# Top-4 routing by top-8 instructions, its marks and ranks moved to GpSimd, the shared expert moved between the first maxima, and the first attention unit's operands loaded early

## The reference, cut to what matters

```python
xn = layernorm(x)
s = attention_block(xn)            # two 8-head attentions of head width 8, then a feed-forward
# gate over 32 experts in 8 groups of 4
scores = softmax(xf @ wg.T)                                # (4096, 32)
keep_g = the 4 groups with the largest group maximum
masked = where(keep_g, scores, -inf)
_, idx = top_k(masked, 4);  w = scores[idx] / (sum + 1e-9)
oh = one_hot(idx.reshape(-1), 32)
pos = (cumsum(oh, axis=0) * oh).sum(-1) - 1                # rank of a token within its expert
keep = pos < cap                                           # cap = 640 rows per expert
y = scatter-add over experts of ((silu(xe@w1) * (xe@w3)) @ w2) * w
z = (silu(xf @ sw1) * (xf @ sw3)) @ sw2                    # the shared expert, all tokens
x = x + s * silu(y + z)
```

## Time and profile before

| what | us |
|---|---|
| median of 3 runs | 1955.45 (1953.72 to 1958.94) |
| the profiled execution, its own time | 1959.3 |
| its span, first to last instruction | 1957.4 |
| first chunk of maxima, PE | 117.6 |
| first score of the attention, PE | 148.65 |
| last exponentials of the attention, about | 1335 |

### The profile page before, as it was taken

The page is one execution under the profiler, slowest core; times in us unless marked ns, Lnnn a source line. Parts: engine busy times, 40 slices in busy tenths (PEclk is TensorE's granted clock), DMA queues, the critical chain, the costliest instruction groups (busy, mean ns, idle before and its releaser), DMA issues.

```text
span 1957.4 us, 41209 instructions
## 1 busy us (share of the span) xinstructions
PE 1756.8 (90%) x15446; PEld 661.8 (34%) x15446; DVE 1684.3 (86%) x2501; ACT 1522.4 (78%) x2880; POOL 422.0 (22%) x676
## 2 busy tenths in 40 slices
...
DMA packets 156349, 146.35 MB, mean 75 GB/s; under 512 B 39882, under 2 KB 135117, under 8 KB 156002
## 3 DMA queue, kind: packets, MB, share of 16 engines
...
## 4 chain that ended last, share of the span: by engine, by line
PE 70%; DVE 10%; ACT 9%; POOL 5%; issue 5%; DMA 1%; SPq 0%; POOLq 0%; DVEq 0%; ACTq 0%
PE PS L1770 28%; PE PS L1796 16%; PE PS L1754 10%; POOL VP L1628 4%; ACT probs L1243 4%; PE PS L1839 4%; ACT SG L1232 2%; PE PS L2034 2%; PE PS L2016 2%; DVE mxp L808 1%; PE PS L1826 1%; DVE YM L892 1%; PE PS L2106 1%; PE PS L2037 1%; PE PS L2019 1%
## 5 line engine op out<-in xcount | busy, mean ns | idle before, releaser
L808 DVE TENSOR_REDUCE mxp<-PS 128x1 f32<-128x1024 f32 x1024 | 1169.1, 1212 | 16.9 <-PE PS L1754 13.4
L1243 ACT ACTIVATE probs<-PS 128x512 f32<-128x512 f32 x2048 | 1095.8, 596 | 86.7 <-PE PS L1796 38.8
L1770 PE MATMUL PS<-probs,VH 128*32 128x256 f32 x8192 | 655.5, 392 | 35.5 <-ACT probs L1243 21.2
L1754 PE MATMUL PS<-stacks 48*128 48x512 bf16 x2048 | 407.2, 384 | 15.9 <-DVE mxp L808 15.9
L1796 PE MATMUL PS<-stacks 51*128 51x512 bf16 x2048 | 414.1, 388 | 0.0
L1770 PEld LDWEIGHTS PS<-probs,VH 128*32 128x32 f32 x8192 | 162.4, 108 | 469.3 <-ACT probs L1243 240.1
L1796 PEld LDWEIGHTS PS<-stacks 51*128 51x128 bf16 x2048 | 110.0, 93 | 424.3 <-ACT probs L1243 391.1
L1628 POOL DMA_INDIRECT VP<-oe_d,ROWI x128 | 132.8, 1037 | 215.6 <-DMA oe_d<-stacks 172.5
L1597 POOL DMA_INDIRECT xe_d<-xn_s,rows_s x128 | 126.5, 988 | 215.1 <-PE PS L1770 180.4
L1575 POOL CAST spl<-nmx 128x8 bf16<-128x8 f32 x64 | 12.0, 188 | 577.7 <-DVE nmx L803 428.2
L820 DVE TENSOR_TENSOR stacks<-stacks,PS 128x640 f32<-128x640 f32 x32 | 26.2, 819 | 112.4 <-ACT stacks L1281 112.4
...
## 6 DMA issues: line engine op xcount, KB each, us to landing
...
o_d<-SG SPq DMA_DIRECT2D x256, 32.0 KB, 1.9
...
```

The costliest lines, as they stand in the source:

```text
L808: v.tensor_reduce(mxp[:, n // 2, n % 2:n % 2 + 1], MXB[n % 2].rearrange("p a c -> p (a c)"), X_AX, ALU.max).then_inc(mx_done, 1)
L1243: act.activation(probs[:, at:at + 512], PS[:, bank_of(u, e), :], ACT.Exp, scale=float(1.0 / np.sqrt(np.float32(DK)))).then_inc(exp_done, 1)
L1754: mm = pe.matmul(MXB[n % 2][:, i, :], QS[w][o:o + MAXROWS, (n // 2) * P:(n // 2 + 1) * P], KS[w][o:o + MAXROWS, key:key + 512], start=True ...
L1770: mm = pe.matmul(OB[32 * jg:32 * jg + 32, c:c + 256], VH[w][:, kt, :], probs[:, at:at + 256], start=(kt < 2 and half == 0), stop=(kt >= TC ...
```

## The change

The four rounds over 128x1024 become one `max` (the 8 largest, in order) and one `max_index` (their places) for each of the 32 tiles. The tiles of these are spread over the eight remainders. The third part of the keys goes from POOL to DVE (`third`), and its wait is the new semaphore `part2k`. Marks, counts and rows go to POOL, in steps between the `largest` calls of units 0 to 8; the prefix counts on PE (`ranks`, four bf16 matmuls) go into unit 5 at step 21, in the place of one chunk, with an ACT copy behind them. One instruction less of the row work stays on DVE in the experts (a reciprocal and a product of the weights). PE's shared expert is cut into 24 steps, each behind one of the first 26 chunks, and its inputs use the PSUM banks 0 and 1. For unit 0, SP loads the queries after the fourth block's stores, and ACT itself issues the key loads between block 6 and block 7; the units 1, 2 and 3 and the late constants are loaded later, at three places of SP's order.

```diff
+    def store_parts(j):
+        hold(part2k, j + 1)
         hold(part2, j + 1)
         for parts, src, stored in ((ql_d, QPARTS, ql_st), (kl_d, KPARTS, kl_st)):
             hold(stored, 48 * j)
             for lv in range(3):
                 sp.dma_start(parts[lv, :, j * 512:(j + 1) * 512], part(src, lv, j % 4)).then_inc(stored, 16)
...
+    def load_first_queries():
+        hold(ql_st, 48 * NB // 2)
+        for o in (0, 64):
+            row = o
+            for r in range(3):
+                n = 3 - r
+                sp.dma_start(QS[0][row:row + n * DK, :], ql_d[r, 0:DK, 0:S].unsqueeze(0).broadcast_to([n, DK, S])).then_inc(qk_ld[0], 16)
+                row += n * DK
+    for j in range(NB // 2):
+        store_parts(j)
...
+    for j in range(NB // 2, NB):
+        store_parts(j)
...
-    for u in range(4):
-        load_unit(u, u // 2, u % 2, u)
+    load_unit(1, 0, 1, 1)
...
     load_max(0, 0, 0, 0)
+    load_unit(2, 1, 0, 2)
...
+            if isinstance(k, int) and u == 0:
+                load_unit(3, 1, 1, 3)
+            if isinstance(k, int) and u == 1:
+                load_late()
...
+        after(v, part2k, j - 1)
...
+    def third(j):
+        v.wait_ge(part1, j + 1)
+        v.tensor_tensor(part(KPARTS, 2, j % 4), KREST[j % 2], part(KPARTS, 1, j % 4), ALU.subtract).then_inc(part2k, 1)
...
+    remainder(0)
     link(v.tensor_tensor(rank, rank, io[:, 0:NG].unsqueeze(1).broadcast_to([P, NT, NG]), ALU.subtract))
...
+    remainder(1)
     link(v.tensor_tensor(g4(M), g4(SC), keep, ALU.min))
...
-    for k in range(KTOP):
-        ek, wk = (t[:, :, k:k + 1].broadcast_to([P, NT, E]) for t in (EK, WK))
-        link(v.tensor_reduce(WK[:, :, k:k + 1], M.unsqueeze(2), X_AX, ALU.max))
-        link(v.tensor_tensor(hots[4], M, wk, ALU.is_equal))
-        link(v.tensor_tensor(hots[4], hots[4], exps, ALU.mult))
-        remainder(2 * k)
-        link(v.tensor_reduce(EK[:, :, k:k + 1], hots[4].unsqueeze(2), X_AX, ALU.min))
-        link(v.tensor_tensor(hots[k], exps, ek, ALU.is_equal))
-        link(v.scalar_tensor_tensor(flat(M), flat(hots[k]), -4.0, flat(M), ALU.mult, ALU.add))
-        if k < KTOP - 1:
-            remainder(2 * k + 1)
-    v.tensor_scalar(SEL, M, -2.5, None, ALU.is_lt).then_inc(sel_done, 1)
-    remainder(NB - 1)
...
-    v.wait_ge(lg_ready, 3)
-    link(v.tensor_copy(T1, bank(2)))
-    v.sem_inc(sums_read, 1)
-    src, dst = T1, SC
-    step = 1
-    while step < NT:
-        link(v.tensor_copy(dst[:, 0:step, :], src[:, 0:step, :]))
-        link(v.tensor_tensor(dst[:, step:NT, :], src[:, step:NT, :], src[:, 0:NT - step, :], ALU.add))
-        src, dst, step = dst, src, 2 * step
...
-    for k in range(KTOP):
-        link(v.tensor_tensor(T1, hots[k], M, ALU.mult))
-        link(v.tensor_reduce(ROW[:, :, k:k + 1], T1.unsqueeze(2), X_AX, ALU.add))
...
+    for j in range(2, NB):
+        third(j - 2)
+        if j < 4:
+            for t in range(NT // 2 * (j - 2), NT // 2 * (j - 1)):
+                ins = v.max(top8[:, t, :], M[:, t, :])
+            link(ins)
+        else:
+            for t in range(NT // 4 * (j - 4), NT // 4 * (j - 3)):
+                v.max_index(place8[:, t, :], top8[:, t, :], M[:, t, :])
+        remainder(j)
+    third(NB - 2)
...
+            if n == 0 and uu == 0:
+                third(NB - 1)
...
+        v.wait_ge(rows_done, 1)
+        link(v.reciprocal(s0, s0))
+        link(v.tensor_tensor(WK[:, :, :], WK[:, :, :], s0.unsqueeze(2).broadcast_to([P, NT, KTOP]), ALU.mult))
...
+    def load_first_keys():
+        act.wait_ge(kl_st, 48 * NB // 2)
+        for o in (0, 64):
+            row = o
+            for r in range(3):
+                n = 3 - r
+                act.dma_start(KS[0][row:row + n * DK, :], kl_d[0:n, 0:DK, 0:S]).then_inc(qk_ld[0], 16)
+                row += n * DK
...
+        if j == NB - 2:
+            load_first_keys()
...
+            if u == RANK_UNIT and e == RANK_EXP:
+                act.wait_ge(lg_ready, 3)
+                act.activation(place.rearrange("p t e -> p (t e)"), MXB[RANK_CHUNK % 2].rearrange("p a c -> p (a c)"), ACT.Copy).then_inc(sums_read, 1)
...
-        for left, parts in ((QREST, QPARTS), (KREST, KPARTS)):
-            ins = pool.tensor_tensor(part(parts, 2, j % 4), left[j % 2], part(parts, 1, j % 4), ALU.subtract)
-        ins.then_inc(part2, 1)
...
+        pool.tensor_tensor(part(QPARTS, 2, j % 4), QREST[j % 2], part(QPARTS, 1, j % 4), ALU.subtract).then_inc(part2, 1)
...
+    def chosen(k):
+        rlink(pool.tensor_tensor(hot_t, numbers, EK[:, :, k:k + 1].broadcast_to([P, NT, E]), ALU.subtract))
+        rlink(pool.tensor_scalar(hots[k], hot_t, 0.0, None, ALU.is_equal))
+    def chosen_any():
+        rlink(pool.tensor_tensor(hot_t, hots[0], hots[1], ALU.add))
+        rlink(pool.tensor_tensor(hot_t, hot_t, hots[2], ALU.add))
+        rlink(pool.tensor_tensor(taken.rearrange("p (t e) -> p t e", e=E), hot_t, hots[3], ALU.add))
+        rlink(pool.memset(before[:, 0:E], 0.0))
+    def counted(half):
+        for t in range(1 + 15 * half, 16 + 16 * half):
+            rlink(pool.tensor_tensor(before[:, t * E:(t + 1) * E], before[:, (t - 1) * E:t * E], taken[:, (t - 1) * E:t * E], ALU.add))
+        if half == 1:
+            pool.sem_inc(cum_done, 1)
+    def fold(src, into):
+        n = E // 2
+        while n > 1:
+            rlink(pool.tensor_tensor(hot_t[:, :, 0:n], src[:, :, 0:n], src[:, :, n:2 * n], ALU.add))
+            src, n = hot_t, n // 2
+        rlink(pool.tensor_tensor(into, hot_t[:, :, 0:1], hot_t[:, :, 1:2], ALU.add))
+    def row_of(k):
+        if k == 0:
+            pool.wait_ge(sums_read, 1)
+        rlink(pool.tensor_tensor(hot_t, hots[k], place, ALU.mult))
+        fold(hot_t, ROW[:, :, k:k + 1])
...
     for u in range(3):
         values(u)
+    for j in range(6):
+        gated_product(j)
     largest(0, 0)
+    for j in range(6, NB):
+        gated_product(j)
+    begin_rows()
...
+    def rows_step(n):
+        if n < KTOP:
+            chosen(n)
+        elif n == KTOP:
+            chosen_any()
+        elif n <= KTOP + 2:
+            counted(n - KTOP - 1)
+        elif 2 * RANK_UNIT + 2 <= n < 2 * RANK_UNIT + 2 + KTOP:
+            row_of(n - 2 * RANK_UNIT - 2)
+        elif n == 2 * RANK_UNIT + 2 + KTOP:
+            end_rows()
     for u in range(3, UNITS // 2):
         values(u)
         largest(u - 3, 1)
+        rows_step(2 * (u - 3))
         largest(u - 2, 0)
+        rows_step(2 * (u - 3) + 1)
...
+    def shared(m):
+        j, step = divmod(m, 3)
+        if step < 2 and j < NB:
+            shared_in(j, step)
+        elif step == 2 and 0 < j < NB:
+            shared_project(j - 1)
+        elif m == CHUNKS + AHEAD - 1:
+            shared_project(NB - 1)
...
+    def ranks():
+        pe.wait_ge(cum_done, 2)
+        pe.wait_ge(mx_done, RANK_CHUNK - 1)
+        for h in range(2):
+            pe.matmul(MXB[RANK_CHUNK % 2][:, h, :], upto16, taken[:, h * 512:(h + 1) * 512], start=True, stop=False)
+            mm = pe.matmul(MXB[RANK_CHUNK % 2][:, h, :], ones16, before[:, h * 512:(h + 1) * 512], start=False, stop=True)
+        mm.then_inc(lg_ready, 1)
...
+    pe.wait_ge(ew_ld[0], 16)
+    pe.wait_ge(v_out, NB)
     for m in range(CHUNKS + AHEAD):
         max_chunk(m)
-        if m == CHUNKS // 2:
-            pe.wait_ge(rows_done, 1)
+        shared(m)
...
+            if u == RANK_UNIT and e == RANK_EXP:
+                ranks()
+            elif u == RANK_UNIT and e == RANK_EXP + 1:
+                pass
+            elif chunk < min(CHUNKS * UNITS, CHUNKS * (u + 1) + AHEAD + CHUNKS * (e + 1) // EXPS):
                 max_chunk(chunk)
```

131 lines of the change are left out of this document (67 added, 64 removed).

## The result

The changed kernel took 1931.56 us (median of 4 executions, 1928.95 to 1936.8), the kernel before 1955.23 us beside it: ratio 0.9874, 95% interval 0.9859 to 0.9889. It is faster by 23.7 us, where 41.8 were forecast, and it lies 1.6 us above the upper end of the range.

The account below looks back on a forecast made before the run. DVE's list and the first maxima were taken to bound the stretch before a full attention. Terms -47.7 + 2.0 + 1.0 + 1.7 + 0.7 - 1.0 + 1.5 = -41.8 us gave a forecast of 1913.5 us, range 1902 to 1930.

Parts of the forecast that it names:

- the landing of the first operands: Before the first chunk: unit 0's key loads land near 70.5, queries near 69, so the first chunk can go at 72.
- Rival (c): Unit 0's loads wait at the end of the stores; the first chunk comes 8 us later, 1921; chance 0.08.
- a cold PE: In the first 26 chunks PE was said to idle no longer, so its clock should be high, over 0.8.
- chunk pitch: In the first 26 chunks, each was taken at 1.20 us against 1.12 before: 25 x 0.08 = +2.0.
- the eighth third: The keys' last subtraction on DVE, between the first two reductions of maxima, was taken to add +1.0 us.
- rival (a): PE paces the first maxima at 1.55 us a chunk, +8.8; with max_index at 0.5 us as well, 1932; chance 0.15.
- The start of the attention: At the first score: ACT's exponential table costs +0.7 us, a warm PE gives -1.0 us.
- DVE's list: From 41.22 to the first reduction: remainders 11.2, thirds 7.0, top-8 instructions 10.2, sum 31.3 us, DVE ready at 72.5.
- Rival (b): Every third finds GpSimd's subtraction just started and waits: +14.6 us, so 1928; chance 0.06.
- the attention's cover: In units 0 to 8, GpSimd's row work of about 67 us, in steps of at most 8, costs nothing.
- (d): GpSimd's 128x1024 instructions cost double and nine steps in units 0 to 8 delay the maxima: +27, 1940; chance 0.06.
- (e): GpSimd's steps stop DVE's reductions in units 0 to 8, up to 67 us, 1980, slower than before; chance 0.03.

Follow-up runs that it names:

- d1: The changed kernel with SP issuing all twelve loads of unit 0 and ACT none: 1931.96 us, ratio 0.9869 to the kernel before.
- k1: The changed kernel with unit 0's loads reading the feature rows outermost and the copies inside: 1929.36 us, ratio 0.9859 to the kernel before.
- w1_warm: The changed kernel with 14 matmuls that nobody reads on PE in front of the first chunk: 1929.73 us, ratio 0.9862 to the kernel before.
- e1_tables: The changed kernel with one-element Silu and Exp instructions so that ACT's tables load ahead: 1929.18 us, ratio 0.9845 to the kernel before.
- p2_best: The changed kernel with rows-outermost loads for unit 0, 10 unread matmuls and both tables ahead: 1920.03 us, ratio 0.9805 to the kernel before.
- a2_again: The changed kernel, unaltered, on another chip: 1933.92 us, ratio 0.9875 to the kernel before.
- p1_best: The changed kernel with rows-outermost loads for unit 0, 14 unread matmuls and both tables ahead: 1994.97 us, ratio 0.986 to the kernel before.
- m1: The changed kernel with rows-outermost unit 0 loads, all from SP, top-8 instructions later, eight shared-expert steps before the first chunk, tables early: 1929.1 us, ratio 0.9856.
- b1: The changed kernel with the early load undone, unit 0 loaded behind all stores, the keys' last third ahead of the first reduction: 1946.39 us, ratio 0.9942.

## Why the prediction was wrong, step by step

**The step that failed: the landing of the first operands.** The prediction had the six key loads land 2 us behind their last issue, at 70.5. The last landed at 76.80, 7.45 us behind the start of the last issue and 7.0 behind its end (69.79). The 2 us are what stores take (2.0 us, the median of the kernel before), which use most of the engines: from 60.00 to 61.70, with stores alone under way, the share is 0.77. These loads use 2 to 3 of 16 (d1), and with the other order of dimensions they land in 4.25 us and the first chunk stands at 72.40 (k1), where the prediction had put it (72). The key stores' landing (65.17, forecast 65) and the end of ACT's issues (4.60 us on its timeline, taken 3.7; ACT is free at 69.9, forecast 68.5) were close. Nothing in the prediction looked at the DMA share of the loads before, though a window of the kernel before shows it, in which nothing but loads of units moved:

```profile
120.00:130.00 10.00, 4.34 (x16) 0.82 (x16) 9.93 (x12) 0.00 (x0) 0.00 (x0) 0.55 0.20 71
```

Rival (c) had priced such a lateness at +8 and 1921, but for another reason, a wait at the end of the stores. What it left out is what followed.

**The sequel that the prediction excluded: a cold PE.** It said that PE no longer idles and its clock would be high. PE idled for 12.76 us and ran at the lower level for 14. The first six intervals between chunks took 14.4 us, and 9.2 in w1_warm, which runs the same work in the same order: the clock cost 5.2. In both of them PE also waits some 1.5 us for ACT, which loads the Silu table (1.28 us), a cost that stands in no term of the sum; e1_tables, without the load there, still waits 0.70. That the clock stays low for 14 us is not certain either: in e1_tables it was back after some 4.

**The chunk pitch was mis-sized.** Taken 1.20, measured 1.38 to 1.41 at a clock of 1.00 (an f32 step 1.06 to the next start, a chunk 0.32). The 19 intervals at the full clock take 25.3 us where 19 x 1.20 = 22.8 were taken, +2.5 (18 of them hold a step; the last, without one, is 0.3 us long). The six before them take 9.2 at the full clock (w1) where 7.2 were taken, +2.0, of which 1.5 is the wait for ACT. With 5.2 for the clock and 0.3 from the last chunk to the score, less the 1.0 of the eighth third, which is hidden now that PE paces, it makes 9.0, and 13.9 - 4.7 = 9.2 were missing. It is rival (a), about half-way to its 1.55: PE paces the first maxima. The range took in half of this rival. Its sign in the profile is there, DVE with gaps in the 26 chunks and PE without: from 91.40 to 117.60 PE is busy 25.75 of 26.20 us and DVE 22.82. The rival's time, 1932, is the measured one only by coincidence, since its other half, a slow max_index, did not occur.

**The start of the attention.** Taken +0.7 for the table and -1.0 for a warm PE; it was +1.5. The first exponential starts 1.26 us behind the first score, since ACT loads the table only then; PE idles 1.08 us behind the first scores, and the granted clock is 0.63 in the 9 us behind the first score. In p2_best, with the table ahead, the first exponential follows the first score by 0.42 us in place of 1.26, the granted clock is 0.81 in the first 9 us, and the stretch takes 21.66 us, 1.8 less than in a2_again (23.46).

**Right, DVE's list.** Remainders 1.40 a block, six of the first seven thirds 0.68 to 0.69 and the seventh 1.46, 1.4 us less than the 7.0 taken, and the top-8 instructions cheaper than taken. DVE's timeline:

```profile
48.31 1.58 DVE L794 MAX8 top<-probs 128x8 f32<-128x32 f32 x16
...
55.57 0.07 DVE L798 MATCH_VALUE_LOAD place<-top,probs 128x8 f32 x1
55.63 0.19 DVE L798 FIND_INDEX8 place<-top,probs 128x8 uint32<-128x32 f32 x1
...
71.22 1.41 DVE L751 SCALAR_TENSOR_TENSOR waq<-PS,bcol,stacks 128x512 f32<-128x512 f32 x2 [4.82 <-ACT stacks L1220]
72.54 1.46 DVE L756 TENSOR_TENSOR stacks<-waq,stacks 128x512 bf16<-128x512 f32 x1
77.69 1.23 DVE L812 TENSOR_REDUCE mxp<-PS 128x1 f32<-128x1024 f32 x1 [3.69 <-PE PS L1854]
```

A max is 0.10 us (taken 0.12). A max_index is two instructions, one every 0.16 us (taken 0.20): 32 of each are 8.3 us, not 10.2. DVE then waits 4.82 us for ACT and 3.69 for the first chunk, so none of what it saved counts. Rival (b), the port, fell: only the third at 72.54 began inside a GpSimd subtraction (72.30 to 73.45), and it cost 0.77 us. Beside the third at 47.70, which began first, the subtraction at 48.11 took 1.30 us instead of 1.16. The rival's price was too high as well: undisturbed, a GpSimd subtraction takes 1.16 us here, and the 2.14 of the earlier trace rows were its length beside the DVE list of the kernel before.

**Right, the attention's cover.** GpSimd's row work stayed hidden. By its lines it is 61 us (67 taken); GpSimd's sum rose by only 38, since eight of its sixteen thirds went to DVE and the others take 1.16 us instead of up to 2.14. Its timeline, and all reductions of maxima by the tile's view:

```profile
169.57 1.96 POOL L1638 TENSOR_TENSOR waq<-io,EK 128x1024 f32<-128x1024 f32 x1
171.62 2.78 POOL L1639 TENSOR_SCALAR XNT<-waq 128x1024 f32<-128x1024 f32 x1
...
207.00 2.35 POOL L1642 TENSOR_TENSOR waq<-XNT 128x1024 f32<-128x1024 f32 x1
```

```profile
L812 DVE TENSOR_REDUCE mxp<-PS x1024: 1208/1214/1226, 77.7 to 1280.2; 128x1 f32<-128x1024 f32 x171
```

The reductions are as they were the earlier trace rows, and the half units keep their 18.25 and 18.77 us while GpSimd works: rivals (d) and (e) fell. Only unit 5 has one half of 20.70 for 18.76, +1.9 (taken 1.5); DVE's gap is in front of the chunk put off:

```profile
320.98 1.03 ACT L1271 ACTIVATE waq<-PS 128x1024 f32<-128x1024 f32 x1
...
322.59 2.36 DVE L812 TENSOR_REDUCE mxp<-PS 128x1 f32<-128x1024 f32 x2 [2.16 <-PE PS L1854]
```

**The end.** The stretch behind the last half unit's output differs by 2.7 us between the two profiles. Over the sixteen profiles of whole kernels other than p1_best's it goes from 619.3 to 625.8, and the unaltered changed kernel alone executes in 1928.94 to 1937.68 us. That scatter is as large as the gains of w1, e1, k1 and m1 at the first score (4 to 7 us), whose medians (1929.1 to 1929.7) are 0.4 to 4.8 us below the changed kernel's three (1930.11, 1931.56, 1933.92). In the profiled executions the gains do arrive: against the changed kernel's 1934.7 the spans are shorter by 11.3 (w1), 8.6 (m1), 7.3 (k1) and 4.5 us (e1), each at least its gain at the first score. But the changed kernel's profiled execution is the longest of its four in each of its three sets, by 0.5 to 6.7 us. Whether the whole of such a gain reaches the end in every execution stays open. That an earlier start as such reaches the end is shown by p2_best (9.6 us at the first exponential, 13.9 in the median) and by b1 (13.9 at the first score, 14.8 in the median).
